# One order of work in the token mixer, one bank plan in the convolution, and two query products instead of four in retention

## The reference, cut to what matters

```python
# token block: B=64 batches, T=125 steps, C=128 channels, H=4 heads, K=31 taps, HID=512
logits = (x @ Wl.T + bl).reshape(B, T, H, K)       # masked at the borders
w = softmax(logits)                                 # the taps
y = einsum('bthk,btkhd->bthd', w, x_gathered) + bias
z = conv1d(y, Wc) + bc                              # 31 taps, 95 steps out, 512 channels
h = selu(z) @ W2.T + b2
# retention block, 8 heads of 16
q, k, v = einsum(xh, wq), einsum(xh, wk), einsum(xh, wv)      # complex
scores = einsum('bhse,bhte->bhst', q, k) * decay
y = einsum('bhst,bhte->bhse', scores, v).real       # then a norm over each head
out = silu(x @ w1) * norm(y) @ w2                   # added to the input
```

## Time and profile before

| what | us |
|---|---|
| median of 3 runs | 2396.18 (2394.02 to 2402.12) |
| the profiled execution, its own time | 2397.24 |
| its span in the trace | 2395.4 |
| mixer, first band product to first spectral product | 26.29 to 158.83 |
| convolution, to its last instruction | 158.83 to 460.62 |
| retention, to the first instruction of the mixture behind it | 460.62 to 757.94 |

### The profile page before, as it was taken

The page is one execution under the profiler, slowest core; times in us unless marked ns, Lnnn a source line. Parts: engine busy times, 40 slices in busy tenths (PEclk is TensorE's granted clock), DMA queues, the critical chain, the costliest instruction groups (busy, mean ns, idle before and its releaser), DMA issues. The chain is left out here.

```text
span 2395.4 us, 43279 instructions
## 1 busy us (share of the span) xinstructions
PE 2081.8 (87%) x14951; PEld 1484.8 (62%) x14951; DVE 1619.7 (68%) x3612; ACT 1198.7 (50%) x2015; POOL 912.8 (38%) x763
## 2 busy tenths in 40 slices
PE   6899999799995999999999989999999994777660
PEld 5777888555553666666666646777777773565450
DVE  5526544467774888888888865676676665666663
ACT  2434433345541766767667656565565552332330
POOL 0000000024432778778777770000000001776772
PEclk9999999899996999999999999999999995667995
DMA  8841000089501000000000000000000002214554
GB/s 286 328 161 36 28 19 2 19 351 419 231 2 71 1 1 1 0 0 0 0 0 0 0 20 1 1 0 0 0 0 0 0 1 59 77 43 134 167 145 158
DMA packets 64710, 165.38 MB, mean 69 GB/s; under 512 B 12450, under 2 KB 43476, under 8 KB 55100
## 3 DMA queue, kind: packets, MB, share of 16 engines
q1 hardware_dynamic: 51580, 148.24, 17.3%
q0 software_dynamic: 7104, 12.71, 1.6%
q10 hardware_dynamic: 5888, 2.62, 0.4%
HBM read 68.62 MB, written 96.86 MB: 69 GB/s over the span
## 5 line engine op out<-in xcount | busy, mean ns | idle before, releaser
L1279 POOL TENSOR_TENSOR c_both<-c_hid 128x512 f32<-128x512 f32 x384 | 491.8, 1288 | 144.2 <-ACT c_hid L1252 106.9
L1252 ACT ACTIVATE c_hid<-c_scaled,c_b 128x1024 f32<-128x1024 f32 x384 | 437.1, 1150 | 173.4 <-DVE c_scaled L1326 159.0
L1326 DVE TENSOR_TENSOR c_scaled<-c_p_h,c_shares 128x1024 f32<-128x1024 f32 x384 | 454.4, 1214 | 79.5 <-PE c_p_h L1195 78.7
L1200 PE MATMUL c_p_o<-c_both,c_w 128*128 128x512 f32 x768 | 390.8, 592 | 0.0
L1193 PE MATMUL c_p_h<-c_x_hi,c_w_hi 128*128 128x512 f32 x384 | 291.7, 760 | 2.6 <-DVE c_w_lo L1349 2.6
L642 POOL TENSOR_TENSOR d_ln_rstd<-d_ln_var,d_ln_power 128x2 f32<-128x2 f32 x48 | 33.4, 696 | 528.0 <-DVE d_ln_var L638 528.0
L1200 PEld LDWEIGHTS c_p_o<-c_both,c_w 128*128 128x128 f32 x768 | 144.4, 188 | 35.9 <-issue 2.2
L1510 PEld LDWEIGHTS d_p_s<-d_kk,d_q_bd 128*128 128x128 f32 x768 | 124.0, 192 | 45.9 <-issue 45.9
L1194 PE MATMUL c_p_h<-c_x_lo,c_w_hi 128*128 128x512 f32 x384 | 152.3, 397 | 0.0
L1195 PE MATMUL c_p_h<-c_x_hi,c_w_lo 128*128 128x512 f32 x384 | 151.8, 395 | 0.0
L1512 PE MATMUL d_p_s<-d_q_rows,d_q_sq 128*128 128x128 f32 x768 | 148.5, 275 | 0.0
(11 more groups left out here) (327 smaller groups left out, 4564.0 us busy)
## 6 DMA issues: line engine op xcount, KB each, us to landing
slots<-b_blank SPq DMA_DIRECT2D x56, 1040.0 KB, 23.7
band_scratch<-a_work SPq DMA_DIRECT2D x16, 1024.0 KB, 5.4
a_work<-band_scratch SPq DMA_DIRECT2D x16, 1023.5 KB, 7.6
e_wb<-e_weights SPq DMA_DIRECT2D x63, 164.0 KB, 2.4
a_raw<-in_Wc SPq DMA_DIRECT2D x16, 512.0 KB, 3.8
e_xb<-slots SPq DMA_DIRECT2D x63, 130.0 KB, 2.2
e_yb<-e_again SPq DMA_DIRECT2D x12, 512.0 KB, 5.6
a_work<-in_x_tok SPq DMA_DIRECT2D x16, 256.0 KB, 3.0
```

Source lines behind the costliest of these rows:

```text
L1200: nc.tensor.matmul(p_o[s][:, 0:N], w2[:, q, :], both[q % SLOTS][:, :], start=(q == 0), stop=(q == NQ - 1)).then_inc(s_down, 1)
L1252: nc.scalar.activation(hid[q % SLOTS][:, :, :], scaled[q % SLOTS][:, :, :], ACT.Gelu, bias=b1[:, q:q + 1]).then_inc(s_ge, 1)
L1279: nc.gpsimd.tensor_tensor(both[q % SLOTS][:, :], hid[q % SLOTS][:, 0, :], hid[q % SLOTS][:, 1, :], ALU.add).then_inc(s_bo, 1)
L1326: v.tensor_tensor(scaled[q % SLOTS][:, :, :], p_h[q % SLOTS][:, 0:N].unsqueeze(1).to_broadcast([128, 2, N]), shares[s][:, :, :], ALU.mult) ...
```

## The change

Three edits. In the mixer a batch's `taps` stand two batches behind its `spread` instead of one, with three `gt` buffers instead of two; PE's `logits` stand ahead of `weights` instead of behind them; ACT's `exps` stand one `g_out` later; SP loads `x_tok` behind the two band transfers instead of ahead of them. In the convolution `to_time` alternates between two banks (`p_A[1]` and `p_y`), `turn` uses only `p_A[0]`, `project` stands three groups behind instead of two, z has three buffers, and DVE's order in a group is `add_h`, `selu`, `weights_out` instead of `weights_out`, `selu`, `add_h`. In retention two query products (`NQ = 2`) with undivided score weights take the place of four; ACT writes each of them to `tq` twice, once times a column that is 1 on even heads and once times one that is 1 on odd heads.

```diff
-        work = sb("work", [128, 13760])
+        work = sb("work", [128, 14260])
...
-        gt = [carve(T, HK, NF2) for s in range(2)]
+        gt = [carve(T, HK, NF2) for s in range(3)]
...
-        z = [carve(128, GB * SP) for s in range(2)]
+        z = [carve(128, GB * SP) for s in range(3)]
...
-        p_conv, p_out = p_y, p_log
+        p_turn, p_conv, p_out = p_A[0], [p_A[1], p_y], p_log
...
             for g in range(NG):
-                if 2 <= g - 2:
-                    load_xtok(g - 2)
                 write_band(g)
                 if g >= 1:
                     read_band(g - 1)
                 if g == 2:
                     load_raw(2)
+                if 2 <= g - 2:
+                    load_xtok(g - 2)
                 if 2 <= g and g + 2 < NG:
                     load_xT(g + 2)
                 if g == 10:
                     load_raw(3)
+            read_band(NG - 1)
             load_xtok(NG - 2)
-            read_band(NG - 1)
             load_xtok(NG - 1)
...
-                                            x_tok[g % 2][0:T, n, 32 * h:32 * h + 32], gt[b % 2][:, h, :],
+                                            x_tok[g % 2][0:T, n, 32 * h:32 * h + 32], gt[b % 3][:, h, :],
...
+                if i == 1 and o > 0:
+                    pe.wait_ge(s_rz, NG * o - 1)
...
-                if g >= 2:
-                    pe.wait_ge(s_zt, k - 1)
+                if g >= 1:
+                    pe.wait_ge(s_zt, k)
                 for n in range(GB):
-                    last = nc.tensor.transpose(p_A[g % 2][0:NF2 + 1, n * 128:(n + 1) * 128], zs[:, g * GB + n, :],
+                    last = nc.tensor.transpose(p_turn[0:NF2 + 1, n * 128:(n + 1) * 128], zs[:, g * GB + n, :],
...
-                if k >= 1:
-                    pe.wait_ge(s_rz, k)
+                if k >= 2:
+                    pe.wait_ge(s_rz, k - 1)
                 for n in range(GB):
-                    last = nc.tensor.matmul(p_conv[:, n * SP:(n + 1) * SP], zt[g % 2][:, n, :], idft[:, :],
+                    last = nc.tensor.matmul(p_conv[g % 2][:, n * SP:(n + 1) * SP], zt[g % 2][:, n, :], idft[:, :],
...
             for g in range(NG):
                 spread(g, 0)
                 if g > 0:
+                    taps(g - 1, 2)
+                spread(g, 1)
+                if g > 0:
                     taps(g - 1, 3)
+                if g + AHEAD < NG:
+                    logits(g + AHEAD)
                 if g % 2 == 0:
                     weights(g // 2)
-                spread(g, 1)
+                spread(g, 2)
                 taps(g, 0)
-                if g + AHEAD < NG:
-                    logits(g + AHEAD)
-                spread(g, 2)
+                spread(g, 3)
                 taps(g, 1)
-                spread(g, 3)
-                taps(g, 2)
+            taps(NG - 1, 2)
             taps(NG - 1, 3)
             pe.wait_ge(s_late, LATE)
             for o in range(NO):
                 for i in range(NBK):
                     product(o, i)
-                    if i == 0 and o > 0:
-                        project(o - 1, NG - 1)
+                    if i in (0, 2) and o > 0:
+                        project(o - 1, NG - 2 + i // 2)
                 for g in range(NG):
                     turn(o, g)
                     if o < NO - 1 and g % 2 == 0:
                         weights(CHUNK * (o + 1) + g // 2)
                     if g > 0:
                         to_time(o, g - 1)
-                    if g > 1:
-                        project(o, g - 2)
+                    if g > 2:
+                        project(o, g - 3)
                 to_time(o, NG - 1)
-                project(o, NG - 2)
+                project(o, NG - 3)
+            project(NO - 1, NG - 2)
             project(NO - 1, NG - 1)
...
-                if b >= 2:
-                    act.wait_ge(s_ymm, b - 1)
-                nc.scalar.copy(gt[b % 2], p_A[b % 2][0:T, 0:HK * NF2].rearrange("t (h f) -> t h f", h=HK)).then_inc(s_gt, 1)
+                if b >= 3:
+                    act.wait_ge(s_ymm, b - 2)
+                nc.scalar.copy(gt[b % 3], p_A[b % 2][0:T, 0:HK * NF2].rearrange("t (h f) -> t h f", h=HK)).then_inc(s_gt, 1)
...
-                nc.scalar.copy(zt[g % 2], p_A[g % 2][0:NF2 + 1, :].rearrange("j (n o) -> j n o", n=GB)).then_inc(s_zt, 1)
+                nc.scalar.copy(zt[g % 2], p_turn[0:NF2 + 1, :].rearrange("j (n o) -> j n o", n=GB)).then_inc(s_zt, 1)
...
             for g in range(NG):
                 g_out(g, 0)
+                g_out(g, 1)
                 if g > 0:
                     spectrum_out(g - 1)
-                g_out(g, 1)
+                g_out(g, 2)
                 if g + AHEAD < NG:
                     exps(g + AHEAD)
-                g_out(g, 2)
                 g_out(g, 3)
...
             def selu(o, g):
                 k = NG * o + g
                 dve.wait_ge(s_ez, k + 1)
-                v.tensor_scalar(rz[g % 2], p_conv[:, 0:N].rearrange("o (n s) -> o n s", n=GB), -SELU_ALPHA,
+                v.tensor_scalar(rz[g % 2], p_conv[g % 2][:, 0:N].rearrange("o (n s) -> o n s", n=GB), -SELU_ALPHA,
                                 -SELU_ALPHA, ALU.add, ALU.max).then_inc(s_rz, 1)
                 dve.wait_ge(s_rz, k + 1)
-                if k >= 2:
-                    dve.wait_ge(s_omm, k - 1)
-                v.scalar_tensor_tensor(z[g % 2].rearrange("o (n s) -> o n s", n=GB), ez[g % 2], SELU_ALPHA, rz[g % 2],
+                if k >= 3:
+                    dve.wait_ge(s_omm, k - 2)
+                v.scalar_tensor_tensor(z[k % 3].rearrange("o (n s) -> o n s", n=GB), ez[g % 2], SELU_ALPHA, rz[g % 2],
...
             for o in range(NO):
                 if o > 0:
+                    add_h(o - 1, NG - 4)
                     selu(o - 1, NG - 1)
-                    add_h(o - 1, NG - 2)
+                    add_h(o - 1, NG - 3)
                 for i in range(1, NBK, 2):
                     z_out(o, i)
-                    if i == 1 and o > 0:
-                        add_h(o - 1, NG - 1)
+                    if i in (1, 3) and o > 0:
+                        add_h(o - 1, NG - 2 + i // 2)
                 for g in range(NG):
+                    if g > 3:
+                        add_h(o, g - 4)
+                    if g > 0:
+                        selu(o, g - 1)
                     if o < NO - 1:
                         weights_out(CHUNK * (o + 1) + g // 2, 2 + g % 2)
-                    if g == 0:
-                        continue
-                    selu(o, g - 1)
-                    if g > 1:
-                        add_h(o, g - 2)
+            add_h(NO - 1, NG - 4)
             selu(NO - 1, NG - 1)
+            add_h(NO - 1, NG - 3)
             add_h(NO - 1, NG - 2)
             add_h(NO - 1, NG - 1)
...
-        score_w = sb("score_w", [128, 4, 128])
+        score_w = sb("score_w", [128, 2, 128])
+        half = sb("half", [128, 2])
...
-        NQ = 4
+        NQ = 2
...
                     if i < NQ:
-                        nc.scalar.copy(tq[s][:, :, i, :], p_p[i % 2][:, 0:N].rearrange("p (n s) -> p n s", n=GB))\
-                            .then_inc(s_projc, 1)
+                        for a in range(2):
+                            last = nc.scalar.activation(tq[s][:, :, 2 * a + i, :],
+                                                        p_p[i % 2][:, 0:N].rearrange("p (n s) -> p n s", n=GB),
+                                                        ACT.Identity, scale=half[:, a:a + 1])
+                        last.then_inc(s_projc, 1)
                         continue
...
-            act.wait_ge(s_zero, 5)
+            act.wait_ge(s_zero, 4)
+            act.wait_ge(s_const, CONST)
...
-            v.memset(score_w[:, :, :], 0.0).then_inc(s_zero, 1)
...
-            dve.wait_ge(s_zero, 5)
-            for a in range(2):
-                for r in range(2):
-                    heads = "p (j a d) -> p j a d"
-                    last = v.tensor_copy(score_w[:, 2 * a + r, :].rearrange(heads, a=2, d=RD)[:, :, a, :],
-                                         p_p[r][:, 0:128].rearrange(heads, a=2, d=RD)[:, :, a, :])
+            for r in range(2):
+                last = v.tensor_copy(score_w[:, r, :], p_p[r][:, 0:128])
...
+    side = np.arange(128) // RD % 2
+    d["half"] = f(np.stack([side == 0, side == 1], 1).astype(np.float32))
```

More of the change, by code:

```diff
@@ L356, in project @@
                     pe.wait_ge(s_h, k)
-                nc.tensor.matmul(p_out[:, 0:N], w2[:, o, :], z[g % 2], start=True, stop=True).then_inc(s_omm, 1)
+                nc.tensor.matmul(p_out[:, 0:N], w2[:, o, :], z[k % 3], start=True, stop=True).then_inc(s_omm, 1)
             pe.wait_ge(s_first, FIRST)
@@ L448, in exp_z @@
                     act.wait_ge(s_z, k - 1)
-                nc.scalar.activation(ez[g % 2], p_conv[:, 0:N].rearrange("o (n s) -> o n s", n=GB), ACT.Exp,
+                nc.scalar.activation(ez[g % 2], p_conv[g % 2][:, 0:N].rearrange("o (n s) -> o n s", n=GB), ACT.Exp,
```

(5 more changed lines are left out.)

## The result

The changed kernel takes 2424.36 us (median of 4 runs, 2419.98 to 2426.82) against 2397.77 (4 runs, 2394.02 to 2402.12) for the kernel before on the same chip: ratio 1.0112, interval 1.0098 to 1.0126. It is slower by 26.6 us. The forecast was 2411, +14.5. The profiled execution took 2422.84, its span is 2421.0.

What follows compares the result with a forecast made beforehand. It took the mixer as bound by the loop through `x_T`, the way back by DVE's late copy, retention by DVE and POOL. +3 - 3.5 + 23.5 - 8.5 = +14.5 us on 2396.2 gave 2411, range 2397 to 2424.

Steps and rivals of the forecast that it cites:

- the copy behind `selu`: Way back: DVE's weights copy, now late, holds up PE's next `weights`; about +1.05 us a pair.
- Mixer +3: Mixer: PE's waits on ACT go, but a loop through `x_T` binds; +3 us, bounds -11 and +10.
- The loop: Mixer: `logits`, moved `weights`, DVE's taps, band write, `x_T`, next `logits`; 16.5 us a pair with idle queues, 17.1 taken.
- The clock: Mixer: PE's new waits lower the clock in one or two pairs, up to 1.7 us each; +2 us.
- `x_tok` ahead of `x_T`: Mixer: its transfer, now between band and `x_T`, adds some 0.3 us to the loop, estimated by size.
- the pair of 17.1: Mixer: a pair of groups takes 17.1 us against 16.7 before; five pairs give +2.
- Three slices +23.5: Way back: late weights copy lengthens pairs to 7.0 us; 7.9 us a slice, +23.5 in all.
- The slice's edge: Way back: `to_time` no longer waits but one more `project` stands among the products; taken as nothing.
- Last slice -3.5: Convolution's last slice: second bank frees it from the ring, 2.2 us a group against 2.46; -3.5 us for 14 groups.
- Retention -8.5: Retention: groups 0.45 us shorter, -6.7, and the phase's beginning some -2; -8.5 us, bounds -23 and -2.
- Rival 2: Forecast plus slow clock in mixer and way back: 1.7 us more per mixer pair, +8, 2419; chance 0.12.
- Rivals 3 and 4: 3: mixer or retention gains 11 to 14 us, 2397 to 2400, chance 0.18; 4: way back's copy hidden, 2379, chance 0.08.

Runs made afterwards that it cites:

- e1_mixer: The kernel before with the change's mixer edits alone: 2407.06 us against 2396.68, ratio 1.0043.
- e4_weights_ahead: The kernel before with the mixer's edits alone, but the product of weights ahead of the logits again: 2391.88 us, ratio 0.9979 against the kernel before.
- e5_xT_first: The kernel before with the mixer's edits alone, but SP issues `x_T` ahead of the band's write and read: 2381.11 us against 2397.67, ratio 0.9934.
- e8_filler: The kernel before with the mixer's edits alone, plus 16 useless PE matmuls per even group in the wait for `x_T`: 2400.77 us, ratio 1.0011.
- e2_way_back: The kernel before with the convolution edits alone, DVE's weights copy behind `selu`: 2423.51 us, ratio 1.0116 against the kernel before.
- e11_between: The kernel before with the convolution edits alone, but weights copy ahead of `selu` and `add_h` between `selu`'s two instructions: 2439.78 us against 2465.86, ratio 0.9907.
- e3_retention: The kernel before with the retention edits alone: 2389.76 us, ratio 0.9971 against the kernel before.
- e6_copy_first: The kernel before with the convolution edits alone, but DVE's weights copy ahead of `selu`: 2391.89 us against 2397.67, ratio 0.9970.
- e10_after_copy: The whole changed kernel, but DVE's weights copy ahead of `selu` again: 2453.53 us against 2465.86 for the kernel before, ratio 0.9954.

## Why the prediction went as it did

The direction was right, and so was the main mechanism, the copy behind `selu`. The size failed: +26.6 for +14.5. By stage of the changed kernel the mixer is 9.2 us above its term, the three slices 4.2 and the last slice 0.6; retention is 1.9 below, and the stages that no edit touches make -0.7.

**Mixer +3: this step failed.** `e1_mixer` measured +10.4, and the mixer of the changed kernel takes 12.2 us more, above even the upper bound of +10. The loop was named rightly: `taps` no longer wait for ACT, even `logits` wait for `x_T`, and undoing either link of the loop (`e4_weights_ahead`, `e5_xT_first`) removes 15 to 27 us. Two numbers inside it were off, and a third was right without having been looked at.

- The clock. The prediction took the lower clock for "one or two" pairs, +2. In the changed kernel `weights` run at it, wholly or nearly so, in every one of six pairs, and `logits` wholly or in part in five. Both lie in the loop that the wait closes. `e8_filler` prices it at 4 to 7 us in `e1_mixer`. With it taken out, +3.1 is left (+4.1 by stage), where the prediction's terms without the clock were +2, +0.7 and -1.6, that is +1.1.
- `x_tok` ahead of `x_T`: taken as 0.3 us by its size. It is 0.92, its time on SP's queue (1.82 from write to `x_T`'s issue against 0.90 before). That is most of what parts the pair of 17.1 that I took from the 17.8 measured at full clock.
- `x_tok` behind the band's write: not seen at all. `x_tok` carries a wait for `taps`, and in the earlier trace rows, continued, the band's write came 1.16 us after DVE was done. My sum had no such wait between DVE and the write. For the changed kernel that is right (0.02 to 0.03 us), but by luck: it is the edit that takes the wait away.

The changed pair then sums up: 7.9 from `logits` to the write by my working, which `e8_filler` shows at full clock (7.91 in most pairs); 1.5 more on average at the lower clock; 1.82 to `x_T`'s issue; and 7.9 on average from the issue to `logits`. That is 19.1, measured 19.2.

**Three slices +23.5.** Measured +25.0 alone and +27.7 in the changed kernel. Of a slice 7.96 us come by the next slice's first product, where I had 7.9; pairs are 6.94 where I had 7.0; the wait of 1.4 is there (1.08 + 0.33), the larger piece ahead of `project` rather than `weights`, since `add_h` is queued behind that same late `selu`. The slice's edge, taken as nothing, costs 0.4. The 2.7 us that the changed kernel has on top lie in one place of the third slice, at 377.09: `weights` after a wait of 2.17 us took 2.09 us there, and the `to_time` behind them 2.02, the lower clock again; in the two other slices, and in all three of `e2_way_back`, the same wait left the clock up.

**Last slice -3.5.** Measured -2.9; 2.3 us a group in place of 2.2. What I did not see is that every second `project` still waits 0.44 us for `add_h`; `e11_between` takes that out, but for three waits at the end, and gets 4.2 us more.

**Retention -8.5.** Measured 8.6 less in the stage of `e3_retention` (-6.9 in the median) and 10.4 in the changed kernel. The group went from 15.73 to 15.23, 0.50 where I had 0.45, and DVE still waits for POOL, 3.31 us for 3.68. Of the 1.8 us between the two traces 1.3 lie in one place: the first products of values took 3.56 us in `e3_retention` and 2.30 in the changed kernel.

**The rivals.** Rival 2 was the slow clock, +8 in the mixer at 1.7 us a pair, with chance 0.12, and it came out in the mixer, but in the way back at one place only. What I held against it, that waits of 1 us before left the clock as it was, spoke of waits of another length: the new ones are 1.7 to 4.2. The one row with a wait as long as that, had shown the lower clock, and it should have had the greater weight. Rivals 3 and 4 are out. Rival 4's rule, that independent groups rotate through PSUM banks (the Trainium skill, Perfetto Trace Analysis, Matmuls), agrees with `e11_between`, where the copy stands ahead of `selu` and `add_h` within it: 21.2 us less; that the banks and not the order give them is not shown. In the three slices of the changed kernel the two banks could not pay, because DVE's order held up the next product of weights. That ScalarE and VectorE take their queue strictly in order (the Trainium skill, TensorE: Matmul & The Clock Gate, Architectural detail) agrees with `e2_way_back` and `e6_copy_first`: the place of one copy in DVE's order is all that differs between them, and it is worth 32.6 us.

## What to carry to other kernels

Before moving an instruction, find the loop through other engines and transfers that its result closes, and count the moved work's whole time into it, at the clock that the new wait will bring. A queue entry that carries a wait (a load for a buffer not yet free, a copy of something late) holds everything behind it: put entries in the order in which their waits end, on SP and DVE alike. When extra buffers do not pay, look for the next owner of the bank; here moving one copy and one sum on DVE turned the way back's edits from +26.8 us into -26.1, each against the kernel before on its own chip.

## What the runs showed of the hardware

- Work of no use made the kernel faster: 16 more matmul records in each of six pairs of groups, put into the waits, go with a granted clock of 1.00 in place of 0.91 from 27 to 142 us, and the mixer is 4.5 us shorter for them.
- After waits of 1.6 to 4.2 us for `x_T` `weights` ran at the lower level (2.09 us for 1.17) in most pairs. The same wait does not always bring it: one of 2.17 us was followed by it in one slice of the changed kernel and not in its two others, nor in the three of `e2_way_back`, and `logits` of `e4_weights_ahead` took 1.14 us after a wait of 1.85.
- The time of an issue on SP's queue depends on what stands ahead of it. `x_tok` took 0.33 us as the first of its burst in the kernel before (41.18) and 0.92 as the third in the changed one (85.80).
- The same kernel took 2397 us on some chips and 2466 on others. The traces put the difference into one part of the program: the mixture behind retention and what follows take 1633 to 1638 us on the first and 1693 to 1702 on the others (granted clock 0.92 to 0.93 and 0.90 to 0.91), while the way back is equal: pairs of 5.96 and 5.90 us both in `e6_copy_first` and in `e10_after_copy`. Why the chips differ there is not shown.
